# A graph attention block: counting edges with two sets of slots, and attention heads without GpSimd

## What is computed

```
h = (x @ W).reshape(n, H, C)
e = leaky_relu(alpha_s[src] + alpha_d[dst], 0.2)
e = exp(e - segment_max(e, dst)[dst])
alpha = e / (segment_sum(e, dst)[dst] + EPS)
out = segment_sum(h[src] * alpha[:, :, None], dst)      # 8 heads side by side
h = elu(out + b)                                        # then h @ W2 for the second layer
```

## Time and profile before

| | us |
|---|---|
| median of 3 runs | 1856.82 (1856.78 to 1858.04) |
| the profiled execution, its own time | 1852.02 |
| its span, first to last instruction | 1849.9 |
| counting, first to last product of the windows | 24.5 to 125 |
| main product | 125 to 533.8 |
| heads | 533.8 to 1520.2 |
| second layer and graph convolution | 1520.2 to 1849.9 |

### The profile page before, as it was taken

One profiled execution on the slowest core, in us unless ns is written; L12 is line 12 of the kernel. 1 busy time (PEld: TensorE's weight loads), 2 busy tenths in 40 slices (PEclk: granted clock), 3 DMA queues, 4 the chain that ended last, 5 costly groups with the idle time before them and its releaser, 6 DMA issues. The chain is left out here.

```text
span 1849.9 us, 22198 instructions
## 1 busy us (share of the span) xinstructions
PE 1708.2 (92%) x7573; PEld 1387.4 (75%) x7582; DVE 1283.4 (69%) x2168; ACT 772.0 (42%) x1276; POOL 558.3 (30%) x319
## 2 busy tenths in 40 slices
PE   3779999999989999999999899999999994989998
PEld 1248888878867878777778777788787872878898
DVE  6654445544588877888789778887888428984437
ACT  4213332222345554455345545554455324534240
POOL 0012312212234533354335334434354213320003
PEclk9989999999999999999999999999999996989999
DMA  3015565495564546455555644566454412132123
GB/s 129 1 55 173 188 220 195 160 232 189 171 235 129 191 157 151 133 200 171 177 117 190 196 121 141 188 169 164 126 195 160 156 54 78 52 115 77 52 70 118
DMA packets 133808, 268.02 MB, mean 145 GB/s; under 512 B 23739, under 2 KB 83525, under 8 KB 121029
## 3 DMA queue, kind: packets, MB, share of 16 engines
q1 hardware_dynamic: 133700, 266.63, 45.6%
HBM read 206.21 MB, written 60.40 MB: 144 GB/s over the span
## 5 line engine op out<-in xcount | busy, mean ns | idle before, releaser
L466 POOL TENSOR_TENSOR w2l<-w2r,w2h 128x768 fp32r<-128x768 f32 x96 | 210.7, 2195 | 353.6 <-ACT w2h L587 353.6
L41 PE MATMUL bank<-ph,hc 128*128 128x512 f32 x768 | 300.9, 392 | 11.4 <-DVE mean L877 10.2
L42 PE MATMUL bank<-pl,hc 128*128 128x512 f32 x768 | 300.2, 391 | 0.0
L43 PE MATMUL bank<-ph,hc 128*128 128x512 f32 x768 | 300.1, 391 | 0.0
L753 DVE CUSTOM_DVE_ANT_0 junk<-bank,a_bc 128x512 bf16<-128x512 f32 (+1 forms) x256 | 129.9, 554 | 192.7 <-ACT st L527 176.8
L41 PE MATMUL bank<-hh,w2h 128*128 128x512 f32 x576 | 230.7, 400 | 21.8 <-DVE hl L886 18.3
L462 POOL TENSOR_TENSOR psum_rows<-psum_rows,pf 128x512 f32<-128x512 f32 x96 | 165.8, 1727 | 213.1 <-DVE pf L811 213.1
L41 PE MATMUL bank<-wh,xTh 128*128 128x512 f32 x570 | 224.0, 393 | 5.4 <-POOL wl L452 5.4
L43 PE MATMUL bank<-hh,w2l 128*128 128x512 f32 x576 | 226.5, 393 | 0.0
L42 PE MATMUL bank<-hl,w2h 128*128 128x512 f32 x576 | 226.1, 392 | 0.0
L42 PE MATMUL bank<-wl,xTh 128*128 128x512 f32 x570 | 222.6, 391 | 0.0
(11 more groups left out here) (245 smaller groups left out, 3081.3 us busy)
## 6 DMA issues: line engine op xcount, KB each, us to landing
hc<-h_scratch SPq DMA_DIRECT2D x96, 1024.0 KB, 4.9
h_scratch<-st SPq DMA_DIRECT2D x96, 512.0 KB, 3.0
w2r<-in_L_gnn_W SPq DMA_DIRECT2D x96, 384.0 KB, 4.9
wr<-in_L_gnn_W SPq DMA_DIRECT2D x12, 1536.0 KB, 8.5
gwr<-in_L_gnn_W SPq DMA_DIRECT2D x24, 384.0 KB, 3.3
row_bc<-logits_scratch SPq DMA_DIRECT2D x16, 512.0 KB, 10.5
expo_bc<-expo_scratch SPq DMA_DIRECT2D x16, 512.0 KB, 5.8
xr<-in_x SPq DMA_DIRECT2D x2, 1536.0 KB, 8.2
```

The costliest lines, as they stand in the source:

```text
L41: nc.tensor.matmul(out, sh, mh, start=first, stop=False, skip_group_check=not grouped)
L42: nc.tensor.matmul(out, sh, ml, start=False, stop=False, skip_group_check=not grouped)
L43: return nc.tensor.matmul(out, sl, mh, start=False, stop=last, skip_group_check=not grouped)
L466: nc.gpsimd.tensor_tensor(w2l[:, g % 3, :], w2r[:, g % 3, :], w2h[:, g % 3, :].bitcast(F32), ALU.subtract).then_inc(w2_lo, 1)
```

## The change

Counting: the group of four tiles gives way to a first even tile and a number of pairs. Each window has its own set of ten slots, by the parity of `w`. Eight tiles are written out without a loop and without waits for slots (VectorE waits once for window `w` - 2), the rest comes in a loop of pairs with at least one pass; for these inputs that makes 162 tiles instead of 188. The opening product of zeros goes, except one. Three pieces of x are turned before the first window, the others three windows ahead. They are plain fp32 products with the identity now, not transposes, and TensorE subtracts the rounded part in PSUM with a negative identity (`lessen_x`), so that ScalarE copies the low part and VectorE has no share in it. ScalarE makes 32 tiles of `hot_low` instead of 40, VectorE 96 instead of 88.

Heads: GpSimd does nothing after the first sums. VectorE takes `sum_rows` and `second_low`; the epsilon goes into the first sum. The sum over the partitions takes two products of fp32r parts, for which ScalarE rounds (`sum_high`) and VectorE subtracts (`sum_low`), in place of one fp32 product. `exponents`, and the saving of its results, come at the start of a pass instead of near its end. The gather of the next pass waits for the inverse (`rden_done`), no longer for the addition before it. `second_high` runs two chunks ahead.

```diff
-ACT_TILES = 40
-QT = 4
-EQ = ET // QT
+ACT_TILES = 32
+FIRM = 8
+SLOTS = FIRM + 2
+EP = ET // 2
-    hot_key = put("hot_key", 143360, [P, QT, NB * WD], BF16)
+    hot_key = [put("hot_key0", 143360, [P, SLOTS, NB * WD], BF16), put("hot_key1", 165888, [P, SLOTS, NB * WD], BF16)]
...
@@ SyncE, in the heads
-                    if k == FB - 2 and w < U:
+                    if k == 0 and w < U:
                         save_exponents(w)
                         if w + 1 < U:
-                            sp.wait_ge(logits_out, 64)
+                            if u == 0:
+                                save_logits(3)
+                                sp.wait_ge(logits_out, 64)
                             load_row(w + 1)
...
+                    if k == FB - 2 and w < U:
                         spread_exponents(w)
@@ GpSimd, in the heads
+            for i in range(2, NB):
+                pool.wait_ge(p_full, i + 1)
+                pool.wait_ge(p_sum, i - 1)
+                nc.gpsimd.tensor_tensor(psum_rows[:, :], psum_rows[:, :], pf[:, i % 2, :], ALU.add).then_inc(p_sum, 1)
@@ ScalarE
+            def x_low(g):
+                act.wait_ge(x_less, g + 1)
+                nc.scalar.copy(xTl[:, g % FB, (g // FB) * HALF:(g // FB + 1) * HALF], x_bank(g)[:, :]).then_inc(x_lo, 1)
...
+            def sum_high(v):
+                act.wait_ge(p_sum, v * 7 + 7)
...
+                nc.scalar.copy(psum_h[:, :], psum_rows[:, :]).then_inc(sum_hi, 1)
@@ VectorE, counting
             for w in range(NW):
...
+                if w >= 2:
+                    dve.wait_ge(count_full, w - 1)
+                for j in range(FIRM):
+                    nc.vector.tensor_scalar(hot_key[w % 2][:, j, :], lane[:, :], keyT[:, 0, bass.ds(first + j, 1)], float(-NB * WD * w),
+                                            ALU.subtract, ALU.is_equal).then_inc(hot_ready[w], 1)
+                with dve.Fori(FIRM // 2, pairs) as q:
+                    for j in range(2):
+                        dve.wait_ge(hot_free[w], q * 2 + (j + 1))
+                        nc.vector.tensor_scalar(hot_key[w % 2][:, FIRM + j, :], lane[:, :], keyT[:, 0, bass.ds(q * 2 + first + j, 1)], float(-NB * WD * w),
                                                 ALU.subtract, ALU.is_equal).then_inc(hot_ready[w], 1)
-                for g in X_LOW_AFTER.get(w, ()):
...
-                    nc.vector.tensor_tensor(xTl[to], x_bank(g)[:, :], xTh[to].bitcast(F32), ALU.subtract).then_inc(x_lo, 1)
@@ VectorE, a pass of the heads
-                if more:
-                    weights(v, 0)
-                    weights(v, 1)
-                    if u == 0:
-                        dve.wait_ge(main_full, STEPS)
-                    weight_low(v, 0)
+                if u >= 1:
+                    if w < U:
+                        exponents(w, top_junk[:, :])
+                    second_low(g + 1)
                 average(g)
...
+                    weights(v, 0)
                 head_sum(g)
                 if more:
+                    weight_low(v, 0)
+                head_low(g)
+                if u == 0:
+                    exponents(w, top_junk[:, :])
+                if more:
+                    weights(v, 1)
+                    sum_rows(v, 1)
                     weight_low(v, 1)
+                if u == 0:
+                    second_low(0)
+                    second_low(1)
+                second_low(g + 2)
                 average(g + 1)
@@ TensorE
-                    last = nc.tensor.transpose(x_bank(g)[:, j * P:(j + 1) * P], xr[:, 4 * half + j, f * P:(f + 1) * P], ident[:, :])
+                    last = nc.tensor.matmul(x_bank(g)[:, j * P:(j + 1) * P], xr[:, 4 * half + j, f * P:(f + 1) * P], ident[:, :],
+                                            start=(j == 0), stop=False, skip_group_check=True)
+            def lessen_x(g):
...
+                f, half = g % FB, g // FB
+                pe.wait_ge(x_hi, g + 1)
+                nc.tensor.matmul(x_bank(g)[:, :], neg_ident[:, :], xTh[:, f, half * HALF:(half + 1) * HALF],
+                                 start=False, stop=True, skip_group_check=True).then_inc(x_less, 1)
...
+                for j in range(FIRM):
+                    pe.wait_ge(hot_ready[w], j + 1)
+                    mm = nc.tensor.matmul(bank[:, :], hot_low[:, bass.ds(first + j, 1), :].rearrange("p t l -> p (t l)"), hot_key[w % 2][:, j, :],
+                                          start=(j == 0), stop=False, skip_group_check=True)
+                    if j == 0 and w + 1 < NW:
+                        mm.then_inc(hot_free[w + 1], SLOTS)
...
+                if w < XG:
+                    if w + X_BEFORE < XG:
+                        turn_x(w + X_BEFORE)
+                    lessen_x(w)
...
-                    pe.wait_ge(den_out, u + 1)
+                    pe.wait_ge(rden_done, u + 1)
...
-                nc.tensor.matmul(bank[:, :], ones[:, :], psum_rows[:, :], start=True, stop=True).then_inc(den_full, 1)
+                pe.wait_ge(sum_lo, v + 1)
+                nc.tensor.matmul(bank[:, :], ones_r[:, :], psum_h[:, :], start=True, stop=False)
+                nc.tensor.matmul(bank[:, :], ones_r[:, :], psum_l[:, :], start=False, stop=True).then_inc(den_full, 1)
```

More of the change, by code:

```diff
@@ L258, in graph_and_heads @@
     XG = 2 * FB
-    X_AFTER = {w: (w,) for w in range(XG)}
-    X_LOW_AFTER = {w + 1: (w,) for w in range(XG)}
+    X_BEFORE = 3
     BLOCK_AT = {(b // 2, 1 + 4 * (b % 2)): b for b in range(NB)}
@@ L513, in _ @@
             nc.scalar.copy(gcn_bias1[:, :], banks[4][:, 256 + 2 * FB:256 + 3 * FB]).then_inc(cols_done, 1)
+            for g in range(X_BEFORE):
+                x_high(g)
             for w in range(NW):
@@ L630, in _ @@
                 if more:
-                    weight_high(v, 1)
+                    weight_high(v, 0)
                 head_high(g)
                 if more:
-                    exponentials(v, 3)
+                    exponentials(v, 2)
+                    weight_high(v, 1)
+                if u == 0:
+                    for k in range(3):
+                        second_high(k)
                 bend(g + 1)
@@ L653, in _ @@
                 head_high(g + 3)
+                second_high(g + 4)
                 if more:
+                    exponentials(v, 6)
+                    weight_high(v, 6)
                     exponentials(v, 7)
-                    weight_high(v, 6)
+                bend(g + 4)
+                if more:
                     weight_high(v, 7)
-                second_high(g + 4)
-                bend(g + 4)
                 head_high(g + 4)
+                if more:
+                    sum_high(v)
                 second_high(g + 5)
@@ L663, in _ @@
                 head_high(g + 5)
+                if more:
+                    second_high(g + 6)
+                    second_high(g + 7)
         @block.vector
@@ L861, in _ @@
                         weights(0, b)
+                        if b == 1:
+                            sum_rows(0, 1)
                         if b >= 1:
@@ L865, in _ @@
             logits_of(3)
+            sum_low(0)
+            inverse(0, banks[0])
             logits_turned(3, banks[1])
-            inverse(0, banks[0])
-            dve.wait_ge(rden_done, 1)
             def average(g):
@@ L926, in _ @@
                 head_low(g + 1)
+                if more:
+                    sum_rows(v, 2)
                 average(g + 2)
@@ L936, in _ @@
                 if more:
-                    weights(v, 5)
+                    sum_rows(v, 3)
+                second_low(g + 3)
+                if more:
+                    weights(v, 4)
                     weight_low(v, 4)
+                    sum_rows(v, 4)
                 average(g + 3)
                 if more:
-                    weights(v, 6)
+                    weights(v, 5)
                 head_sum(g + 3)
@@ L946, in _ @@
                 if more:
+                    sum_rows(v, 5)
+                second_low(g + 4)
+                if more:
+                    weights(v, 6)
+                    weight_low(v, 6)
+                    sum_rows(v, 6)
+                average(g + 4)
+                if more:
                     weights(v, 7)
-                    weight_low(v, 6)
+                head_sum(g + 4)
+                if more:
                     weight_low(v, 7)
-                if w < U:
-                    exponents(w, top_junk[:, :])
-                average(g + 4)
-                head_sum(g + 4)
                 head_low(g + 4)
+                if more:
+                    sum_rows(v, 7)
+                    sum_low(v)
+                second_low(g + 5)
                 average(g + 5)
@@ L958, in _ @@
                 if more:
+                    second_low(g + 6)
                     inverse(v, banks[6])
```

166 lines of the change are left out of this document (82 added, 84 removed).

## The result

The changed kernel takes 1778.77 us (median of 4 runs, 1777.28 to 1781.29); the kernel before, beside it, 1856.8 us (4 runs, 1849.07 to 1858.04). The ratio is 0.959, 95% interval 0.9561 to 0.9618. Forecast were 1797 us and a range of 1780 to 1826: the sign was right, 60 us of gain were worked out and 78 came, and the time is just under the range. The profiled execution took 1777.28 us, 74.7 less than the profiled one before; the other 3 us are in the medians, which lie 4.8 above the profiled execution before and 1.5 after.

A forecast was written before the change was run, and what follows sets the result against it. TensorE looked like the bound overall, but counting was held by TensorE and VectorE waiting for each other, and the heads by TensorE's losses. Gains of 28 + 32 = 60 us from 1852.0 gave 1792, plus 4.8 for the median 1797; range 1780 to 1826.

The forecast's parts named there:

- the sum of 4.73 us a window: Counting: TensorE's terms added up for each of the nine windows that still turn a piece of x.
- entry into the loop: Counting: entering the rolled loop costs TensorE what a new group cost, 0.51 + 0.10 = 0.61 us.
- reads of the bounds: Counting: TensorE's reading of the loop's bounds adds 0.99 us to every window.
- The sum for VectorE: Counting: VectorE's keys, group crossing and reads of the bounds add to 3.94 us a window, pacing the other seven windows.
- The rule of the Trainium skill that would have made the piece 1.68: Counting: fp32 transposes four times faster than plain products; the stage's gain would be 21 us instead of 28.
- stretches at 1.2 GHz: Counting: slow-clock stretches in which a tile costs twice 0.22 us; 3 us taken off 31, leaving 28.
- the wait before P0: Heads, first pass: the first projection waits some 11 us for `second_low(0)`, behind the bounds and `weights(1, 1)`.
- why is `head_low` late: Heads: GpSimd's subtraction stretches VectorE's operations, 2.22 us for what takes 0.69; without GpSimd they go back to 0.60 apart.
- the split sum: Heads: the sum over the weights as two fp32r products costs 0.45 us, not 0.87; 15 of them save 6.3.
- Rival 4: Heads: GpSimd's absence changes nothing, stretched operations were hidden; only sums (6) and counting (28) win, 1823 us; chance 0.05.
- Those have 15 us until their gather: Heads, SyncE: three node loads, behind the row load and save moved ahead of them, still have 15 us to spare.
- Rivals 1 to 3: Counting wins half, 1813 us, 0.12; heads win half, 1813 us, 0.12; VectorE becomes the bound, 1879 us, 0.06.

The follow-up runs named there:

- e3_low_on_gpsimd: Changed kernel with the low part of the second weights (`second_low`) given back to GpSimd, in the new order; 1779.43 us, ratio 0.9584.
- e4_first_pass: Changed kernel with rounding and low parts of the first second-layer weights ahead of the first pass's other work, bounds saved behind two more node loads; 1772.16 us, ratio 0.9535.
- e11_slots_without_reuse: Changed kernel with four tiles of a window unrolled instead of eight, and twelve slots a set, one for each tile; 1810.4 us, ratio 0.9692.
- e12_x_low_on_vector: Changed kernel with x's pieces turned by transposes and their low parts made by VectorE's subtraction, as before the change; 1780.6 us, ratio 0.953.
- e5_all_on_gpsimd: Changed kernel with sums 2 to 7 of every head and every `second_low` back on GpSimd, in the new order; 1783.85 us, ratio 0.9539.

## Why the prediction was right, and where it was off

**Counting: the step that failed is the sum of 4.73 us a window.** Its terms, predicted and then read from the window above: eight tiles and the entry into the loop 1.54 + 0.61 = 2.15, measured 1.53 (27.20 to 28.73); second tile and closing product 0.49, measured 0.65; piece of x 0.87, measured 0.89; subtraction 0.23, measured 0.34 with its gap; reads of the bounds 0.99, measured nothing. The sum is 3.41. Two terms carry the miss, the entry (-0.62) and the reads (-0.99). Both had been read from the earlier trace rows as gaps of TensorE and added to its products. They are work of its sequencer, and it lies beside products that are already queued; a gap in the kernel before showed only that nothing was queued there. The Trainium skill says so (Advanced Engine Details and Errata, Sequencer Loop: "Other engine instructions can be read & queued while ucode executes"), and the trace agrees, by the gap of 1.29 without a queued piece against 0.15 with one. The doubled reads show how much is hidden: about 1.3 us a window, and no more.

The sum for VectorE failed in the same way: from the start of a window's last key to the next one's first 1.4 us were forecast, 0.65 measured, and a window takes 3.01 instead of 3.94. Here the longer unrolled row is the cover; with four tiles the gap is back at 1.20.

**Counting: the start and the fp32 products** came as worked out: first load at 23.75 (forecast 23.7), piece of x 0.89 (0.87). The rule of the Trainium skill that would have made the piece 1.68 does not hold here: the plain product takes about twice the transposes' 0.42, not four times.

**Counting: the clock.** 3 us were taken off for stretches at 1.2 GHz; there were none, with the granted clock at 1.00 from 23.75 to 80.06. With some 14.5 us from the windows these 3 make the 17.5 that separate 28 from 45.5. The heads took 2.5 back, and the medians' smaller distance from the profiled execution (1.5, where 4.8 was added) gave 3.3: together the 18 us by which 1797 was too high.

**What counting's gain consists of.** Eight tiles unrolled instead of four are worth 28 us, some 4.6 of them by the clock; the kernel before had none unrolled, but four tiles in a turn, so this is no share of the 45.5. The second set gives 3, the first load 2.1. Moving x's low part to TensorE and ScalarE is worth nothing measurable in this place. What the opening products, the fewer tiles and the clock (0.92 before) gave, no run separates. What bounds a window now is TensorE's sequencer, some 3.35 us of reads, loop and issue: with less array work its reads stayed 3.4 apart, and with a second pair of reads the window grew by all of their time. In the changed kernel the array is close behind, with 3.26 us of its 3.41 filled, so by that sum a shorter sequence alone would win little in the windows with a piece.

**Heads: the size was right, the reason half wrong.** Forecast 32, measured 29.5. Passes of 57.6 us, no wait for `hl`, low parts at 692 ns, VectorE at 703.9 busy us over 15.7 passes, 44.8 a pass (45.2 forecast), the wait before P0 of 10.3 (some 11 forecast): each as written. The last has more to it than the queue of VectorE that the prediction names: by `e3_low_on_gpsimd` ScalarE's rounding alone, behind the same bounds, makes P0 as late. And the answer to "why is `head_low` late" was put down to GpSimd's stretch, and that step fell: with GpSimd's 326 us back, the passes stayed 57.6. The place of the bounds alone is worth 23.6 us; the other 6 of the 29 are the size forecast for the split sum (6.3), which no run takes alone. Rival 4 had the right premise, that GpSimd's absence changes nothing in the passes, and the wrong time, since the order was not in it. That 32 came out near the measured 29.5 is partly luck: the order that was written along with the change brought what had been put down to GpSimd. Whether leaving GpSimd out would help in the old order, no run shows.

**Heads: the missed wait.** "Those have 15 us until their gather" failed once. SyncE's own issues:

```profile
518.78 0.58 SPq L331 DMA_DIRECT2D logits_scratch<-logitT  x1
528.56 0.32 SPq L314 DMA_DIRECT2D row_bc<-logits_scratch  x1
529.05 0.32 SPq L337 DMA_DIRECT2D hc<-h_scratch  x1
```

Between the save of the logits and the load of the row that needs it SyncE stands 9.8 us, and the node load is queued behind it; the gather at 536.8 waits for it 3.5 us. I had counted the issues that were moved ahead, and not the wait among them. `e4_first_pass`, which moves them back behind two node loads in the first pass, has no such wait.

**Rivals 1 to 3.** Counting won more, not half; the heads won all; VectorE was idle 14 us a pass, and in an ordinary pass TensorE waited for nothing of it.

## What to carry to other kernels

A gap that the profile puts down to issue is not a cost of the engine: ask whether its sequencer could have done that work under queued instructions, and price the new code by what will be queued then. Once the array is covered, count the sequencer's own work too: here it became the bound, at 3.35 us a window. A short hardware loop with two tiles in a turn cost more in turns than in tiles (1.04 us against 0.44); write out as many tiles as every case has, and loop over the rest. When a change moves work off an engine and reorders the rest, run the order alone: here the stretched operations were the striking rows, and the block of bounds in the wrong place was the cost. Compare against the spread of kernels that share the part in question: 4 us in one first pass looked like an effect and was not clear of it.

## What the runs showed of the hardware

At a turn of TensorE's rolled loop its weight loads stood idle 0.69 to 0.84 us at full clock with the data ready (`e11_slots_without_reuse`). Two reads of a register from SBUF, 0.3 us each, cost its sequencer with the arithmetic around them about 1.29 us, hidden under queued products (a gap of 0.15) or paid (1.29). The sequencer of TensorE kept its reads 3.4 us apart while the array did two windows in 2.66 us each (`e12_x_low_on_vector`). GpSimd's 512-column addition took 1.63 us on the mean and its 768-column subtraction 1.99 beside a busy VectorE, whose operations stretched from 0.69 to as much as 2.34, and the time of the passes did not move by it (`e5_all_on_gpsimd`).
